# A three-level image synthesis inside a vision-transformer kernel: the coarse products at their own widths, spread in SBUF by GpSimd

## What is computed

```python
img = x[..., 0]
cur = img
for _ in range(3):
    cur, h, v, d = _dwt2(cur)
    details.append((h, v, d))
aw = jax.nn.sigmoid(cur.reshape(B, -1) @ Wa + ba)
rec = cur * aw[:, :, None]
for (h, v, d), (Wd, bd) in zip(reversed(details), det_params):
    w = jax.nn.softmax(jnp.stack([h, v, d], axis=1).reshape(B, -1) @ Wd + bd, axis=-1)
    rec = _idwt2(rec, h * w[:, 0, None, None], v * w[:, 1, None, None], d * w[:, 2, None, None])
...
h = concat([cls_tok, rec], axis=1)
h = h + attention(layernorm(h))      # 16 heads of 64, rotary, ALiBi, causal
h = h + ffn(layernorm(h))            # 256 -> 2 x 1024 -> 256, rounded
```

## Time and profile before

| | us |
|---|---|
| median of 3 runs | 1751.57 |
| lowest, highest | 1749.1, 1755.12 |
| span of the profiled execution | 1750.5 |
| TensorE busy (modelled) | 1664.2 |
| VectorE busy | 1470.0 |
| ScalarE busy | 1323.6 |
| GpSimd busy | 1120.1 |

### The profile page before, as it was taken

The page is one execution under the profiler, slowest core; times in us unless marked ns, Lnnn a source line. Parts: engine busy times, 40 slices in busy tenths (PEclk is TensorE's granted clock), DMA queues, the critical chain, the costliest instruction groups (busy, mean ns, idle before and its releaser), DMA issues.

```text
span 1750.5 us, 48653 instructions
## 1 busy us (share of the span) xinstructions
PE 1664.2 (95%) x16742; PEld 1278.3 (73%) x16742; DVE 1470.0 (84%) x4972; ACT 1323.6 (76%) x3812; POOL 1120.1 (64%) x1034
## 2 busy tenths in 40 slices
PE   7758999999999999999999999999999999999975
PEld 6635777777777777777777777777777777777653
DVE  3837888899888888899888888899888888889874
ACT  0326888888888888888888888888888888888762
POOL 0087667766777666766777667666677667666500
PEclk9789999999999999999999999999999999999986
DMA  9311111111111111111111111111111111111100
GB/s 320 110 61 61 56 53 56 53 67 57 61 68 68 59 61 57 50 65 62 56 68 68 66 55 60 54 56 66 55 64 68 68 53 61 56 53 62 44 7 13
DMA packets 90168, 113.70 MB, mean 65 GB/s; under 512 B 14818, under 2 KB 52163, under 8 KB 89667
## 3 DMA queue, kind: packets, MB, share of 16 engines
q1 hardware_dynamic: 89922, 110.59, 18.1%
HBM read 26.62 MB, written 8.42 MB: 20 GB/s over the span
## 4 chain that ended last, share of the span: by engine, by line
PE 88%; DVE 4%; SPq 3%; POOL 2%; ACT 1%; issue 1%; DMA 0%; DVEq 0%; POOLq 0%; ACTq 0%
PE bank L725 45%; PE bank L842 9%; PE bank L983 7%; PE bank L831 6%; PE bank L829 6%; PE bank L994 3%; PE bank L853 3%; PE bank L903 3%; PE bank L891 2%; PE bank L1003 2%; SPq L320 1%; PE bank L882 1%; DVE arena L1283 1%; PE bank L950 0%; POOL rot L486 0%
## 5 line engine op out<-in xcount | busy, mean ns | idle before, releaser
L482 POOL TENSOR_TENSOR arena<-rq,cos 128x512 f32<-128x512 f32 x256 | 326.1, 1274 | 280.0 <-ACT rq L526 280.0
L535 ACT ACTIVATE arena<-arena,nm 128x129 f32<-128x129 f32 (+1 forms) x1024 | 455.6, 455 | 0.0
L486 POOL TENSOR_TENSOR rot<-rot,sin 128x512 f32<-128x512 f32 x256 | 326.3, 1275 | 103.9 <-DMA rot<-rq 103.9
L725 PE MATMUL bank<-xt_h,weights 128*128 128x256 f16 x2048 | 378.9, 273 | 9.2 <-ACT rq L526 7.8
L526 ACT ACTIVATE rq<-bank,bqk 128x256 f32<-128x256 f32 x512 | 214.4, 471 | 170.1 <-PE bank L725 155.3
L1283 DVE CUSTOM_DVE_ANT_0 arena<-bank,bias 128x129 f32<-128x129 f32 (+1 forms) x1024 | 317.9, 352 | 26.5 <-issue 16.6
L489 POOL TENSOR_TENSOR arena<-arena,rot 128x512 f32<-128x512 f32 x256 | 314.2, 1228 | 37.3 <-POOL rot L486 0.9
L1291 DVE TENSOR_TENSOR ptr_l<-bank,ptr_h 128x384 f16<-128x384 f32 x512 | 280.0, 552 | 31.8 <-ACT ptr_h L545 29.4
L545 ACT ACTIVATE ptr_h<-bank 128x384 f16<-128x384 f32 x512 | 249.1, 486 | 68.6 <-PE bank L725 44.0
L725 PE MATMUL bank<-xt_l,weights 128*128 128x256 f16 x1024 | 279.6, 273 | 0.0
L842 PE MATMUL bank<-eye,arena 128*128 128x128 f32 x1536 | 253.0, 277 | 8.5 <-DVE ptr_l L1291 4.4
(11 more groups left out here) (200 smaller groups left out, 3182.5 us busy)
## 6 DMA issues: line engine op xcount, KB each, us to landing
rot<-rq SPq DMA_DIRECT2D x512, 128.0 KB, 2.0
arena<-in_x SPq DMA_DIRECT2D x4, 2048.0 KB, 15.2
xin<-in_x SPq DMA_DIRECT2D x32, 256.0 KB, 2.8
hr<-hr SPq DMA_DIRECT2D x32, 256.0 KB, 2.3
out<-h SPq DMA_DIRECT2D x64, 128.0 KB, 2.1
arena<-in_L_attn_w_qkv SPq DMA_DIRECT2D x2, 1536.0 KB, 8.6
weights<-in_L_ffn_w_down SPq DMA_DIRECT2D x1, 1024.0 KB, 11.8
arena<-in_L_ffn_w_gate SPq DMA_DIRECT2D x1, 1024.0 KB, 8.5
```

The lines of the kernel that those rows point to most:

```text
L482: pool.tensor_tensor(dst, rq[:, g % 2].rearrange("p j (t n) -> p j t n", t=T), cos[:, :].rearrange("p (t n) -> p t n", t=T).unsqueeze(1).b ...
L486: pool.tensor_tensor(r, r, sin[:, :].unsqueeze(1).broadcast_to([P, 2, SIDE]), ALU.mult).then_inc(t2_ready, 1)
L535: act.activation(cols, cols, ACT.Exp, bias=nm[:, t, h:h + 1], scale=-1.0, accum_out=rs[:, t, h:h + 1]).then_inc(e_done, 1)
L725: ins = pe.matmul(dst, lhs[l], rhs[r], start=start and n == 0, stop=stop and n == len(parts) - 1)
```

## The change

The three coarse products are written side by side into `u_bank`, at 256, 128 and 64 columns, and no longer added there. ScalarE copies all 448 columns to one tile `levels`, of which `pair_sum`, `quad_sum` and `eight_sum` are parts. GpSimd then adds each number of `eight_sum` to two of `quad_sum`, and each of these sums to two of `pair_sum`; VectorE's add waits for the second of these sums by a new semaphore, coarse_spread. The two sums stand behind rotate 4 in GpSimd's queue, and image_rstd moves from behind rotate 5 to behind rotate 6.

```diff
-        pair_sum = sb("pair_sum", [P, T, 128])
+        levels = sb("levels", [P, T * (128 + 64 + 32)])
+        pair_sum, quad_sum, eight_sum = (levels[:, i:j].rearrange("p (t n) -> p t n", t=T) for i, j in ((0, 256), (256, 384), (384, 448)))
...
+            def spread_coarse(a):
+                if not image(a):
+                    return
+                pool.wait_ge(coarse_out_done, a + 1)
+                for i, (fine, wide, n) in enumerate(((quad_sum, eight_sum, 32), (pair_sum, quad_sum, 64))):
+                    if i:
+                        pool.wait_ge(coarse_spread, 2 * a + 1)
+                    pool.tensor_tensor(fine.rearrange("p t (n r) -> p t n r", r=2), fine.rearrange("p t (n r) -> p t n r", r=2),
+                                       wide.unsqueeze(3).broadcast_to([P, T, n, 2]), ALU.add).then_inc(coarse_spread, 1)
...
                 rotate(s + 1, 4)
+                spread_coarse(s + 2)
                 rotate(s + 1, 5)
+                rotate(s + 1, 6)
                 image_rstd(s + 2)
-                rotate(s + 1, 6)
...
-                act.activation(pair_sum[:, :, :].rearrange("p t n -> p (t n)"), u_bank[:, 0:SIDE], ACT.Copy).then_inc(coarse_out_done, 1)
+                act.activation(levels[:, :], u_bank[:, 0:448], ACT.Copy).then_inc(coarse_out_done, 1)
...
-                for o, (src, n) in enumerate(((s1, 128), (s2, 64), (s3, 32))):
-                    rhs = src[:, :, :].rearrange("p t n -> p (t n)")
-                    if o > 0:
-                        rhs = rhs.unsqueeze(2).broadcast_to([P, T * n, 128 // n])
-                    ins = pe.matmul(u_bank[:, 0:SIDE], rowop[:, o + 1, :], rhs, start=o == 0, stop=o == 2)
+                for o, (src, i, j) in enumerate(((s1, 0, 256), (s2, 256, 384), (s3, 384, 448))):
+                    ins = pe.matmul(u_bank[:, i:j], rowop[:, o + 1, :], src[:, :, :].rearrange("p t n -> p (t n)"), start=True, stop=True)
...
-                dve.wait_ge(coarse_out_done, a + 1)
+                dve.wait_ge(coarse_spread, 2 * a + 2)
```

More of the change, by code:

```diff
@@ L247, in vit_layer @@
         x_in, rowop_ready, syn_ready = sem("x_in"), sem("rowop_ready"), sem("syn_ready")
-        coarse_ready, coarse_out_done = sem("coarse_ready"), sem("coarse_out_done")
+        coarse_ready, coarse_out_done, coarse_spread = sem("coarse_ready"), sem("coarse_out_done"), sem("coarse_spread")
         var_ready, rstd_ready, h_ready, hr_ready = sem("var_ready"), sem("rstd_ready"), sem("h_ready"), sem("hr_ready")
@@ L1413, in image_out @@
                 tt(hh[:, :, :].rearrange("p t (n r) -> p t n r", r=2), b_bank[:, :].rearrange("p (t n r) -> p t n r", t=T, r=2),
-                   pair_sum[:, :, :].unsqueeze(3).broadcast_to([P, T, 128, 2]), ALU.add).then_inc(h_ready, 1)
+                   pair_sum.unsqueeze(3).broadcast_to([P, T, 128, 2]), ALU.add).then_inc(h_ready, 1)
             def image_stats(a):
```

## The result

| | before | after |
|---|---|---|
| median, us | 1751.13 | 1983.38 |
| lowest, highest, us | 1749.1, 1755.12 | 1979.37, 1984.35 |
| span of the profiled execution, us | 1750.5 | 1977.6 |
| mean granted clock over it | 0.976 | 0.926 |

The ratio is 1.131 [1.1288, 1.1332]: slower, by 232 us. The forecast was 1975 us. The profiled execution took 1979.37 us.

A forecast was written before the change was run, and what follows sets the result against it. TensorE, never standing still, was taken to bound the kernel. 1750.5 (profile span) + 1.1 (to the median) + 154 (wait) + 68 (clock) + 1 (prologue) = 1975 us; own range 1940 to 2010, chance 0.76; wider range 1885 to 2010.

The forecast's parts named there:

- Coarse, 0.43 to 0.54 saved, counted at nothing: TensorE's narrower coarse products save 0.43 to 0.54 us per image, lost in project(5)'s wait, so counted as 0.
- The copy, 0.55: ScalarE's copy of 448 instead of 256 columns takes about 0.55 us, 0.15 more; counted as 0 inside the longer wait.
- The sums, 1.10: GpSimd's two added sums take together 1.10 us per image, including about 0.08 for the wait between them.
- The wait, 4.83: Project(5) waits for `hh`, which waits for sums queued behind rotate(4): 4.83 us later in image 16, 154 us together.
- Nothing comes sooner although the period is longer: Rotate(3) and rotate(4) start from copies after TensorE's project(3) and project(4), so nothing can pull the sums forward.
- the rival of the shorter queue: GpSimd enters its rotations earlier in the longer period; delay only 2.4 to 3.8 us, some 1915 us; chance 0.08.
- VectorE's lateness adds nothing, or 0.66: VectorE work queued behind the later `hh` adds nothing; otherwise 0.66 us per image, 20 us in all.
- The clock, 2.2: Half clock on TensorE after each of 31 waits costs 2.2 us, 68 us in all (0 to 96).
- wait without the clock: Rival: the clock does not fall at project(5)'s wait, leaving only the 154 us, 1906 us; chance 0.12.
- image_rstd behind rotate(6): 0: Moved later in GpSimd's queue, image_rstd is done by 861, 5 us before VectorE uses it: cost 0.
- The clock row: Sign in the profile after: TensorE's clock row under 9 in most slices.
- `hh`'s idle time: Sign in the profile after: VectorE's idle time before `hh` is released by the GpSimd sums, not by synthesise.

The follow-up runs named there:

- e5: Changed kernel with coarse ahead of project(4), ScalarE's copy ahead of head 7's exponentials, the sums in rotate(3)'s gap, image_rstd back behind rotate(5): 1756.16 us, ratio 1.0018.
- e7: Changed kernel with ScalarE's copy ahead of weights_hi(5), sums in rotate(3)'s gap, image_rstd back behind rotate(5), turn_tokens behind values(4); coarse unmoved: 1741.46 us, ratio 0.9936.
- e1: Changed kernel with the two GpSimd sums one place earlier in its queue, behind rotate(3) instead of rotate(4): ratio 1.0277; runs of 1796.1, 1796.77 and 1810.57 us.
- e2: Changed kernel with 22 unused products of 512 columns on TensorE ahead of project(5), keeping it busy during the wait: 1939.93 us, ratio 1.1072.
- e6: Kernel before, at full width without GpSimd sums, with only coarse moved ahead of project(4) and the copy ahead of head 7's exponentials: 1769.52 us, ratio 1.0092.
- e8: Kernel before, at full width without GpSimd sums, with only ScalarE's copy moved ahead of weights_hi(5) and turn_tokens behind values(4): 1754.96 us, ratio 1.001.
- e4: Changed kernel with the two sums on VectorE ahead of `hh`, and image_rstd back behind rotate(5) in GpSimd's queue: 1817.2 us, ratio 1.037.

## Why the prediction was right

The time came out 8 us above the forecast, through the step on which the forecast rested: the end of rotate(4) in GpSimd's queue sets `hh`, and `hh` sets project(5).

- **Coarse, 0.43 to 0.54 saved, counted at nothing.** Saved: 0.47 per image. Swallowed by the wait, as forecast; e5, e7 and their controls bring it back.
- **The copy, 0.55.** 0.56. It started no earlier. The wait of turn_tokens behind it was sized at 0.1 and measured 0.27; it lay inside the longer wait, where it cost nothing, but in e1, and as a part of e5's loss, it counts.
- **The sums, 1.10.** 1.17 for the pair, 0.07 more, or 2 us in all. The estimate that the prediction worked out from the Trainium skill ("GPSIMD Engine Reference", section "3. Performance versus the Vector engine") was 0.84, further off.
- **The wait, 4.83.** Project(5) of image 16 starts 9.76 us behind coarse where it was 4.76: 5.00 later. 0.07 of the difference is the sums, 0.05 the start of `hh` (0.09 behind the sum, not 0.04), 0.05 rotate(4), which ends 7.75 behind coarse and not 7.70. Over 25 images the shift is -0.47 + 0.27 + 5.37 = 5.17 against the 4.97 (154 / 31) of the forecast, with its late transfers in it.
- **Nothing comes sooner although the period is longer.** Right: the rival of the shorter queue needed a GpSimd free at rotate(4). Its gap is behind the sums (4.53 us), not ahead of them.
- **VectorE's lateness adds nothing, or 0.66.** The step said that what stands behind `hh` follows at the same distance and TensorE has project(5) to do meanwhile. In the change it adds nothing that can be seen, and in e1, at full clock and with VectorE just as late, it adds nothing either: the reason given holds there. In e2 it adds 0.68, near the alternative price. What the step did not look at is how long the rows behind `hh` last: `ve` takes 0.17, 0.43 or 1.12 by what GpSimd does beside it, and the lateness costs only where `ve` is held to the end of a whole product.
- **The clock, 2.2.** 2.15 per image in the distances, as a mean of images that lose about 1.6 and images that lose about 2.6; the two costs that the prediction took it from, 1.7 and 3.1, lie far apart too. The stretch that it read as 6.5 us long is 6.8 by its own rows; the 6.2 under work, by which it was priced, is right. Taking the fall away saves only 1.4, since the 0.68 comes up. The rival "wait without the clock" was priced at 1906; e2, in which the clock stays, took 1939.93, and 31 x 0.68 = 21 us of the difference is what `ve` costs there.
- **image_rstd behind rotate(6): 0.** It ends at 978.28 [the GpSimd rows above], and its user starts 6.3 us later:

```profile
984.54 0.74 DVE L1437 TENSOR_SCALAR xn<-hh,mv,rstd 128x256 f32<-128x256 f32 x2
```

- **Two of the signs were badly chosen.** The clock row was to stand under 9 in most slices, and reads

```profile
PEclk9778999999999999999999999999999999999996
```

9 in 36 of 40 slices. The forecast's own numbers said so: a loss of 2.2 us in 56 leaves a mean near 0.95, and a digit of 9 means 90% or more. The sign that holds is the mean clock in the window, 0.94. And `hh`'s idle time was to be named after the GpSimd sums; the view calls it "issue".

## What to carry to other kernels

An operation that is moved to an engine with idle time costs its place in that engine's queue, not its duration: 1.17 us of sums cost 232 us behind rotate(3) and rotate(4), some 50 behind rotate(3) alone, and nothing inside rotate(3) with ScalarE's copy one place earlier. Look for a gap in which the engine already waits (here for a DMA) and that begins when the input is ready; a saving on the bounding engine shows only when every wait behind it can follow. And before moving the producer earlier, see what it covers where it stands: coarse hid the emptying of a bank, and that is 0.14 of the 0.38 us per image which e6 loses by moving coarse and the copy; e8, which leaves coarse in its place, loses nothing.

## What the runs showed of the hardware that was not expected

- Adds on VectorE with both inputs in SBUF, which take 0.28 and 0.42 us alone, ended 0.15 and 0.28 us behind whatever GpSimd operation was under way when they began, 56 times out of 56 in e4. Next to a GpSimd that is busy with 1.27 us operations, a short VectorE add between SBUF tiles costs up to 1.48 us.
- A VectorE row of two numbers per partition, with one input in SBUF (`ve`), is held in the same way. In images 5 to 29 of the kernel before, e1 and e2, 73 of 75 began while a GpSimd operation was under way, and 72 of these ended 0.02 to 0.03 us behind its end, after up to 1.26 us; where none was under way, as in all 25 of the changed kernel, it took 0.17.
- The same idle time of 5.05 us is not followed by the same stretch of half clock: in image 16 the clock falls at 964.4, just before the work comes back, and is full at 967.8; in image 20 it falls at 1186.3, in the middle of the wait, and is full at 1193.1 (worked out from the shares in the windows above). Under work that is 3.3 us in the one and 3.7 in the other, so these two pay nearly the same price (1.53 and 1.72 us); over images 5 to 29 the half clock under work goes from 2.8 to 6.0 us, and the price from 1.34 to 2.84. In images 5 to 29 of e1, the stops of 1.20 to 1.74 us were followed by full clock; of the other three, of 2.02, 2.13 and 2.29 us, the first two were followed by half clock and the third was not.
